# Attention cores of a transformer kernel: ScalarE exponentiates one head of eight straight from PSUM, VectorE shifts the other seven

## The chip, the cores and the metric

One core of a Trainium2 chip runs the whole program. The metric is the device time of one launch, in microseconds (us). The engines are TensorE (PE, with its weight loads shown apart as PEld), VectorE (DVE), ScalarE (ACT), GpSimd (POOL) and SyncE (SP). They run beside each other and are ordered only by semaphores. Each works its own instructions in program order.

## What is computed

The program takes 16 sequences of 128 tokens with 256 features through four layers. Each layer has an attention-like step and a feed-forward step. Two of the attention steps, that of layer 0 (causal self-attention, 4 key/value groups for 16 heads) and that of layer 1 (cross-attention to the context, 16 heads), use the function that is changed. Cut to what matters, with 16 heads of 16 features each:

```
scores = einsum('bqhd,bkhd->bhqk', q, k) / sqrt(16)      # layer 0 adds a causal mask of -1e9
attn   = softmax(scores, axis=-1)
out    = einsum('bhqk,bkhd->bqhd', attn, v)
```

The softmax is computed with the row's maximum subtracted before the exponential.

## The kernel before

`attention_core` is called twice: with the tag `l0a` and `causal=True` (the layer-0 stage, about 97 to 216 us of the span) and with the tag `l1a` and `causal=False` (the layer-1 stage, about 712 to 816 us). One call walks through 32 steps, `h` = 0 to 31. A step is half of one sequence's heads: 8 heads, each a 128x128 block of scores, 1024 columns in two PSUM banks. Steps alternate between two pairs of banks (`both(h)`, `bank(h, half)`).

For a step, in the order of the data:

- GpSimd writes `KBD` (L525): the keys of one chunk, repeated four times and multiplied by a 0/1 mask of heads, `C_HEAD`.
- TensorE, `scores(h)`: in the causal stage two matmuls that put the mask into the banks (L545), then two products with the queries, recorded as four matmuls (L548). It waits for `KBD` and, as the bank pair is used again every second step, for the shift of step h-2.
- VectorE, `largest(h)` (L609): the negated maximum of each head into `NM`. `shift(h)` (L616): scores plus that, from PSUM into the SBUF tile `E` (a ring of four).
- ScalarE: the exponential in place in `E` (L666), with the scale 1/4.
- TensorE, `turn(h)`: eight transposes of `E` into PSUM (L558). ScalarE, `copy(h)` (L651): these out of PSUM into `PT`. TensorE, `values(h)` (L572): 16 small matmuls with the values.
- Once for two steps: ScalarE `columns(b)` (L657) copies the sums out of PSUM, TensorE `turn_rows(b)` (L584) transposes them, VectorE `sums` (L624) and `norm` (L629) divide.

The order on each engine is written out by hand. It is what the work around the change hangs on:

- TensorE, iteration h: `scores(h)`; on even h from 6 on `turn_rows((h-6)/2)`; `turn(h-3)`; `values(h-4)`.
- VectorE, iteration h: `largest(h)`, [`sums`], `shift(h)`, [`norm`]; the ones in brackets on even h.
- ScalarE, iteration h: `copy(h-2)`; on even h from 4 on `columns((h-4)/2)`; the exponential of h.

So on ScalarE the exponential of step h-2 stands behind `copy(h-4)`, which waits for `turn(h-4)`; and on TensorE `turn(h-4)` and `values(h-5)` are the last things before `scores(h)`.

Of the kernel before, what the change touches and what calls it, by code (L numbers as in the profile page):

```python
# [23 lines left out]
P = 128  # L24
# [29 lines left out]
def shape_constants():  # L54

    c = np.zeros((P, C_END), np.float32)
    t = np.arange(P)
    c[:, C_IDENT:C_IDENT + P] = np.eye(P)
    lag = t[None, :] - t[:, None]
    c[:, C_DECAY:C_DECAY + P] = np.where(lag >= 0, DECAY ** np.maximum(lag, 0).astype(np.float64), 0.0)  # L60
    half = D // 2
    power = 10000.0 ** (np.arange(half, dtype=np.float32) / np.float32(half)).astype(np.float64)
    theta = np.float32(1.0) / power.astype(np.float32)
    ang = t[:, None].astype(np.float32) * theta[None, :].astype(np.float32)
    c[:, C_COS:C_COS + half] = np.cos(ang.astype(np.float64))
    c[:, C_SIN:C_SIN + half] = np.sin(ang.astype(np.float64))
    c[:, C_CAUSAL:C_CAUSAL + P] = np.where(t[None, :] > t[:, None], NEG_CAUSAL, 0.0)
    c[:, C_LESS:C_LESS + P] = t[:, None] < t[None, :]
    c[:, C_HEAD:C_HEAD + 4] = (t[:, None] % 64) // DH == np.arange(4)[None, :]
    c[:, C_IOTA:C_IOTA + 16] = np.arange(16)[None, :]  # L70
    c[:, C_ROW:C_ROW + 8] = (t[:, None] % 64 - np.arange(8)[None, :]) / 8.0
    return c
# [16 lines left out]
def build(nc, I, out):  # L89
# [20 lines left out]
    with top:  # L110
# [381 lines left out]
        def attention_core(tag, QT, KT, V, AO, groups, causal):  # L492
# [5 lines left out]

            with ExitStack() as c:
                ER, PR, KR = 4, 2, 3  # L500
                KBD = sb_in(c, f"{tag}_KBD", [P, KR, 4, P])
                E = sb_in(c, f"{tag}_E", [P, ER, 2 * BANK])
                PT = sb_in(c, f"{tag}_PT", [P, PR, 2 * BANK])
# [14 lines left out]
                with nc.Block() as block:  # L518
# [14 lines left out]
                    @block.tensor  # L533
                    def _(pe):
                        if causal:
                            pe.wait_ge(s_cm, 1)

                        def scores(h):
                            b, chunk = h // 2, h % 2
                            pe.wait_ge(s_kbd, h + 1)  # L540
                            if h >= 2:
                                pe.wait_ge(s_shift, h - 1)
                            if causal:
                                for half in range(2):
                                    nc.tensor.matmul(bank(h, half), IDB[:, :], CM[:, :, :], start=True, stop=False)  # L545
                            for half in range(2):
                                rows = slice(64 * half, 64 * half + 64)
                                ins = nc.tensor.matmul(bank(h, half), QT[rows, chunk, b * S:(b + 1) * S],  # L548
                                                       KBD[rows, h % KR, :, :], start=not causal, stop=True)
                            ins.then_inc(s_s, 1)  # L550

                        def turn(h):

                            pe.wait_ge(s_exp, h + 1)
                            if h >= 1:
                                pe.wait_ge(s_pt, h)
                            for n in range(8):
                                ins = nc.tensor.transpose(TP[:, n * P:(n + 1) * P],  # L558
                                                          E[:, h % ER, n * P:(n + 1) * P], IDENT)
                            ins.then_inc(s_turn, 1)  # L560

                        def values(h):

                            b, chunk = h // 2, h % 2
                            pe.wait_ge(s_pt, h + 1)
                            if h == 0:
                                pe.wait_ge(s_clear, 1)
                            if chunk == 0 and b >= 1:
                                pe.wait_ge(s_os, b)
                            for n in range(8):  # L570
                                head, slot, at = 8 * chunk + n, 2 * chunk + n // 4, 32 * (n % 4)
                                ins = nc.tensor.matmul(OT[at:at + DH + 1, slot * P:(slot + 1) * P],  # L572
                                                       V[:, b, head * groups // NH, :],
                                                       PT[:, h % PR, n * P:(n + 1) * P],
                                                       start=True, stop=True, skip_group_check=True)
                            ins.then_inc(s_pv, 1)

                        def turn_rows(b):

                            pe.wait_ge(s_os, b + 1)  # L580
                            if b >= 1:
                                pe.wait_ge(s_ao, b)
                            for slot in range(4):
                                ins = nc.tensor.transpose(PS[:, 7, slot * P:(slot + 1) * P],  # L584
                                                          OS[:, slot * P:(slot + 1) * P], IDENT)
                            ins.then_inc(s_row, 1)

                        for h in range(STEPS + 5):
                            if h < STEPS:
                                scores(h)  # L590
                            if h >= 6 and h % 2 == 0:
                                turn_rows((h - 6) // 2)
                            if 3 <= h < STEPS + 3:
                                turn(h - 3)
                            if 4 <= h < STEPS + 4:
                                values(h - 4)

                    @block.vector
                    def _(dve):
                        nc.vector.memset(OT, 0.0).then_inc(s_clear, 1)  # L600
                        if causal:
                            nc.vector.tensor_copy(
                                CM[:, :, :], CONST[:, C_CAUSAL:C_CAUSAL + P].rearrange("p (o s) -> p o s", o=1)
                                .broadcast_to([P, 4, P])).then_inc(s_cm, 1)

                        def largest(h):

                            dve.wait_ge(s_s, h + 1)
                            nc.vector.tensor_reduce(NM[:, h % ER, :], both(h), AX, ALU.max, negate=True).then_inc(s_max, 1)  # L609

                        def shift(h):

                            dve.wait_ge(s_max, h + 1)
                            if h >= ER:
                                dve.wait_ge(s_turn, h - ER + 1)
                            nc.vector.tensor_tensor(  # L616
                                E[:, h % ER, :].rearrange("p (g s) -> p g s", s=P), both(h),
                                NM[:, h % ER, :].rearrange("p (g o) -> p g o", o=1).broadcast_to([P, 8, P]),
                                ALU.add).then_inc(s_shift, 1)

                        def sums(b):

                            dve.wait_ge(s_row, b + 1)
                            nc.vector.reciprocal(RD[:, b % 2, :], O[:, :, DH]).then_inc(s_rd, 1)  # L624

                        def norm(b):

                            dve.wait_ge(s_rd, b + 1)
                            nc.vector.tensor_tensor(  # L629
                                AO[:, b, :].rearrange("p (h e) -> p h e", e=DH), O[:, :, 0:DH],  # L630
                                RD[:, b % 2, :].rearrange("p (h o) -> p h o", o=1).broadcast_to([P, NH, DH]),
                                ALU.mult).then_inc(s_ao, 1)

                        for h in range(STEPS):
                            largest(h)
                            if h % 2 == 0 and h >= 6:
                                sums((h - 6) // 2)
                            shift(h)
                            if h % 2 == 0 and h >= 6:
                                norm((h - 6) // 2)  # L640
                        for b in range((STEPS - 8) // 2 + 1, B):
                            sums(b)
                            norm(b)

                    @block.scalar
                    def _(act):
# [12 lines left out]
                        for h in range(STEPS + 4):  # L659
# [3 lines left out]
                                columns((h - 4) // 2)  # L663
                            if h < STEPS:
                                act.wait_ge(s_shift, h + 1)
                                nc.scalar.activation(E[:, h % ER, :], E[:, h % ER, :], ACT.Exp,  # L666
                                                     scale=DH ** -0.5).then_inc(s_exp, 1)


        def l0_attention():  # L670
# [3089 lines left out]
```

## Time and profile before

| | us |
|---|---|
| median of 3 runs (lowest, highest) | 1597.98 (1592.46, 1606.96) |
| the profiled execution: its own time | 1595.48 |
| its span, first to last instruction | 1593.7 |
| PE, DVE, ACT, POOL busy in the span | 1323.9, 1131.5, 909.3, 719.7 |
| mean granted TensorE clock | 0.912 of full speed |

A time is that of a whole launch; a span is that of the instructions alone. Busy time is summed over the engine's instructions and says nothing of what waits for what; that is read from the stretches in order of time.

### The profile page before, as it was taken

The page shows a single profiled execution, that of the slowest core. Times are in us where ns is not written, and L with a number is a line of the kernel's source. Part 1 is how long each engine was busy: PE and PEld are TensorE (multiplying, and loading weights), DVE is VectorE, ACT ScalarE, POOL GpSimd, SP SyncE. Part 2 cuts the span into 40 slices and gives each one's busy share as a digit, 9 for nine tenths or more (in the row PEclk, how much of TensorE's full clock was granted, in tenths as well). Part 3 has the DMA queues.
Part 4 walks back from the last instruction along what each step waited for, and adds up shares of the span by engine and source line. Part 5 has one row for each costly group of instructions (what it writes and reads, how often), then busy time and mean ns, then how long its engine had stood idle before and what let it go on. Part 6 is the DMA issues. An engine that isn't in the chain of part 4 may idle for free. (4 is left out here: it accounts for less than half of the span.)

```text
span 1593.7 us, 28302 instructions
## 1 busy us (share of the span) xinstructions
PE 1323.9 (83%) x9642; PEld 1110.3 (70%) x9642; DVE 1131.5 (71%) x2469; ACT 909.3 (57%) x1952; POOL 719.7 (45%) x753
## 2 busy tenths in 40 slices
PE   2699977899999999879984679999778965656898
PEld 0445565799999999735564579999776841345687
DVE  6447756688888988559965647898565658785654
ACT  3236652677777877557732348778426357464432
POOL 2223201467766776513320128888402940453444
PEclk8699997999999999899995789999899988676999
DMA  5000003556657666220012216777511000101000
GB/s 187 1 1 1 1 11 118 193 206 262 253 220 267 243 238 256 93 96 1 1 54 93 80 52 247 253 251 251 186 35 54 1 0 1 34 1 62 1 27 27
DMA packets 60780, 173.69 MB, mean 109 GB/s; under 512 B 10256, under 2 KB 42000, under 8 KB 51040
## 3 DMA queue, kind: packets, MB, share of 16 engines
q1 hardware_dynamic: 53152, 151.42, 26.6%
q0 software_dynamic: 7488, 20.46, 3.7%
q8 instruction: 81, 1.33, 0.4%
q14 instruction: 59, 0.48, 0.1%
HBM read 155.34 MB, written 16.52 MB: 108 GB/s over the span
## 5 line engine op out<-in xcount | busy, mean ns | idle before, releaser
L1812 POOL TENSOR_TENSOR l0m_e_DL<-l0m_e_DN,l0m_e_DH 128x256 fp32r<-128x256 f32 x192 | 175.2, 922 | 96.6 <-ACT l0m_e_DH L1655 95.2
L1720 DVE TENSOR_TENSOR l0m_e_UL<-l0m_e_U,l0m_e_UH 128x512 fp32r<-128x512 f32 x192 | 168.7, 884 | 10.9 <-ACT l0m_e_UH L1645 10.4
L1581 PE MATMUL PS<-l0m_e_CH,l0m_e_UH 128*128 128x256 f32 x480 | 138.4, 288 | 2.0 <-DVE l0m_e_CL L1755 2.0
L1581 PE MATMUL PS<-l0m_e_CL,l0m_e_UH 128*128 128x256 f32 x480 | 136.5, 284 | 0.0
L1581 PE MATMUL PS<-l0m_e_CH,l0m_e_UL 128*128 128x256 f32 x480 | 136.5, 284 | 0.0
L1645 ACT CAST l0m_e_UH<-l0m_e_U 128x512 fp32r<-128x512 f32 x192 | 117.9, 615 | 0.0
L1812 POOL TENSOR_TENSOR l1m_e_DL<-l1m_e_DN,l1m_e_DH 128x256 fp32r<-128x256 f32 x96 | 86.9, 921 | 16.6 <-ACT l1m_e_DH L1655 15.5
L1581 PEld LDWEIGHTS PS<-l0m_e_CH,l0m_e_UH 128*128 128x128 f32 x480 | 92.7, 193 | 2.2 <-ACT l0m_e_UH L1645 2.2
L1581 PEld LDWEIGHTS PS<-l0m_e_CH,l0m_e_UL 128*128 128x128 f32 x480 | 92.8, 193 | 0.0
L1581 PEld LDWEIGHTS PS<-l0m_e_CL,l0m_e_UH 128*128 128x128 f32 x480 | 92.8, 193 | 0.0
L1614 PE MATMUL PS<-l0m_e_DH,l0m_e_HH 128*128 128x256 f32 x312 | 89.0, 285 | 4.5 <-issue 2.6
L1720 DVE TENSOR_TENSOR l1m_e_UL<-l1m_e_U,l1m_e_UH 128x512 fp32r<-128x512 f32 x96 | 83.1, 868 | 11.2 <-ACT l1m_e_UH L1645 10.7
L1614 PE MATMUL PS<-l0m_e_DH,l0m_e_HL 128*128 128x256 f32 x312 | 88.6, 284 | 0.0
L1614 PE MATMUL PS<-l0m_e_DL,l0m_e_HH 128*128 128x256 f32 x312 | 88.5, 284 | 0.0
L1655 ACT CAST l0m_e_DH<-l0m_e_DN 128x256 fp32r<-128x256 f32 x192 | 77.8, 406 | 0.2 <-PE PS L1614 0.2
L3505 POOL TENSOR_TENSOR Z<-l3f_WI,Z 128x512 f32<-128x512 f32 x32 | 50.6, 1584 | 59.9 <-DVE Z L3601 54.9
L525 POOL TENSOR_TENSOR l0a_KBD<-l0a_KT,CONST 128x512 f32<-128x512 f32 x32 | 33.4, 1045 | 91.4 <-PE PS L548 62.6
L525 POOL TENSOR_TENSOR l1a_KBD<-CTX,CONST 128x512 f32<-128x512 f32 x32 | 33.1, 1039 | 91.7 <-PE PS L548 48.8
L1734 DVE SCALAR_TENSOR_TENSOR Z<-PS,l0m_e_BU,Z 128x256 f32<-128x256 f32 x120 | 57.3, 478 | 24.2 <-ACT Z L1664 23.8
L1581 PE MATMUL PS<-l1m_e_CH,l1m_e_UH 128*128 128x256 f32 x240 | 70.9, 295 | 2.2 <-DVE l1m_e_CL L1755 1.5
L1746 DVE TENSOR_TENSOR l0m_e_HL<-Z,l0m_e_HH 128x256 fp32r<-128x256 f32 x120 | 70.5, 588 | 0.0
L1664 ACT ACTIVATE Z<-PS,l0m_e_BU 128x256 f32<-128x256 f32 x120 | 56.9, 474 | 23.1 <-PE PS L1581 21.0
(610 smaller groups left out, 4753.5 us busy)
## 6 DMA issues: line engine op xcount, KB each, us to landing
l0m_e_U<-in_l_up SPq DMA_DIRECT2D x24, 2048.0 KB
l0m_e_DN<-in_l_down SPq DMA_DIRECT2D x24, 1024.0 KB
l1m_e_U<-in_l_up SPq DMA_DIRECT2D x24, 1024.0 KB, 6.3
l1m_e_DN<-in_l_down SPq DMA_DIRECT2D x24, 512.0 KB, 3.9
CTX<-in_ctx SPq DMA_DIRECT2D x2, 2048.0 KB, 10.3
l1a_GA<-results_by_choice SPq DMA_DIRECT2D x16, 256.0 KB, 6.0
l1m_c_GA<-results_by_choice SPq DMA_DIRECT2D x16, 256.0 KB, 4.3
Z<-in_l_b_rows SPq DMA_DIRECT2D x24, 128.0 KB, 3.0
```

Of the source, the lines that this page charges most:

```text
L525: nc.gpsimd.tensor_tensor(KBD[:, h % KR, :, :], KT[:, chunk, b * S:(b + 1) * S].rearrange("p (o s) -> p o s", o=1) .broadcast_to([P, 4, S] ...
L1581: ins = nc.tensor.matmul(hb(u)[:, a * SLOTS:(a + 1) * SLOTS], w[:, f % RING, k, a, :], x[:, t % 2, k, :], start=(p == 0), stop=(p == len(p ...
L1614: ins = nc.tensor.matmul(yb(t)[:, r, :], h[:, t % 2, f, r * P:(r + 1) * P], w[:, f % RING, :], start=(f == 0 and r == 0 and p == 0), stop= ...
L1645: nc.scalar.copy(UH[:, f % RING, :, :, :], U[:, t % 2, :, :, f * P:(f + 1) * P]).then_inc(s_uh, 1)
L1655: nc.scalar.copy(DH[:, f % RING, :], DN[:, t % 2, f, :]).then_inc(s_dh, 1)
L1664: ins = nc.scalar.activation(SG[:, u % 4, :], hb(u)[:, 0:SLOTS], ACT.Silu, **kw)
L1720: nc.vector.tensor_tensor(UL[:, f % RING, :, :, :], U[:, t % 2, :, :, f * P:(f + 1) * P], UH[:, f % RING, :, :, :].bitcast(F32), ALU.subtr ...
L1734: ins = nc.vector.scalar_tensor_tensor(out=HR[:, u % 4, :], in0=hb(u)[:, SLOTS:2 * SLOTS], scalar=BU[:, t % 2, 1, f:f + 1], in1=SG[:, u % ...
L1746: ins = nc.vector.tensor_tensor(HL[:, t % 2, f, :], HR[:, u % 4, :], HH[:, t % 2, f, :].bitcast(F32), ALU.subtract)
L1812: nc.gpsimd.tensor_tensor(DL[:, f % RING, :], DN[:, t % 2, f, :], DH[:, f % RING, :].bitcast(F32), ALU.subtract).then_inc(s_dl, 1)
L3505: nc.gpsimd.tensor_tensor(HR(u), HA(u), HB(u), ALU.add).then_inc(s_h, 1)
```

## The change

ScalarE now makes two instructions of the exponential of a step. The first takes the last of the eight heads directly from its PSUM bank, with the negated maximum as its bias (128 columns). The second takes the seven heads that VectorE has shifted (896 columns), in place in `E` as before. VectorE's shift covers seven heads. Both ScalarE instructions stand behind the same wait for the shift of the step, and in the same place of ScalarE's order. The scale 1/4 moves out of the exponential into the head mask `C_HEAD`, and so into `KBD`. Each step counts two on `s_exp`: `turn(h)` waits for both. Since ScalarE now reads the score banks too, `scores(h)` has a second condition for using them again: the first of the two ScalarE instructions of step h-2.

```diff
--- before.py
+++ after.py
@@ -66,7 +66,7 @@
     c[:, C_SIN:C_SIN + half] = np.sin(ang.astype(np.float64))
     c[:, C_CAUSAL:C_CAUSAL + P] = np.where(t[None, :] > t[:, None], NEG_CAUSAL, 0.0)
     c[:, C_LESS:C_LESS + P] = t[:, None] < t[None, :]
-    c[:, C_HEAD:C_HEAD + 4] = (t[:, None] % 64) // DH == np.arange(4)[None, :]
+    c[:, C_HEAD:C_HEAD + 4] = ((t[:, None] % 64) // DH == np.arange(4)[None, :]) * DH ** -0.5
     c[:, C_IOTA:C_IOTA + 16] = np.arange(16)[None, :]
     c[:, C_ROW:C_ROW + 8] = (t[:, None] % 64 - np.arange(8)[None, :]) / 8.0
     return c
@@ -498,6 +498,7 @@
 
             with ExitStack() as c:
                 ER, PR, KR = 4, 2, 3
+                SHIFTED = 7
                 KBD = sb_in(c, f"{tag}_KBD", [P, KR, 4, P])
                 E = sb_in(c, f"{tag}_E", [P, ER, 2 * BANK])
                 PT = sb_in(c, f"{tag}_PT", [P, PR, 2 * BANK])
@@ -540,6 +541,7 @@
                             pe.wait_ge(s_kbd, h + 1)
                             if h >= 2:
                                 pe.wait_ge(s_shift, h - 1)
+                                pe.wait_ge(s_exp, 2 * (h - 2) + 1)
                             if causal:
                                 for half in range(2):
                                     nc.tensor.matmul(bank(h, half), IDB[:, :], CM[:, :, :], start=True, stop=False)
@@ -551,7 +553,7 @@
 
                         def turn(h):
 
-                            pe.wait_ge(s_exp, h + 1)
+                            pe.wait_ge(s_exp, 2 * (h + 1))
                             if h >= 1:
                                 pe.wait_ge(s_pt, h)
                             for n in range(8):
@@ -614,8 +616,8 @@
                             if h >= ER:
                                 dve.wait_ge(s_turn, h - ER + 1)
                             nc.vector.tensor_tensor(
-                                E[:, h % ER, :].rearrange("p (g s) -> p g s", s=P), both(h),
-                                NM[:, h % ER, :].rearrange("p (g o) -> p g o", o=1).broadcast_to([P, 8, P]),
+                                E[:, h % ER, 0:SHIFTED * P].rearrange("p (g s) -> p g s", s=P), both(h)[:, 0:SHIFTED, :],
+                                NM[:, h % ER, 0:SHIFTED].rearrange("p (g o) -> p g o", o=1).broadcast_to([P, SHIFTED, P]),
                                 ALU.add).then_inc(s_shift, 1)
 
                         def sums(b):
@@ -663,8 +665,10 @@
                                 columns((h - 4) // 2)
                             if h < STEPS:
                                 act.wait_ge(s_shift, h + 1)
-                                nc.scalar.activation(E[:, h % ER, :], E[:, h % ER, :], ACT.Exp,
-                                                     scale=DH ** -0.5).then_inc(s_exp, 1)
+                                nc.scalar.activation(E[:, h % ER, SHIFTED * P:8 * P], both(h)[:, SHIFTED, :], ACT.Exp,
+                                                     bias=NM[:, h % ER, SHIFTED:8]).then_inc(s_exp, 1)
+                                nc.scalar.activation(E[:, h % ER, 0:SHIFTED * P], E[:, h % ER, 0:SHIFTED * P],
+                                                     ACT.Exp).then_inc(s_exp, 1)
 
 
         def l0_attention():
```

## Rows read from the trace of the kernel before

**Rows 1.** The page, busy time (share of the span) and instructions of each engine.
```profile
PE 1323.9 (83%) x9642; PEld 1110.3 (70%) x9642; DVE 1131.5 (71%) x2469; ACT 909.3 (57%) x1952; POOL 719.7 (45%) x753
```

**Rows 2.** Windows: stretch, length, then busy time and instruction count of each engine; 15 us of either stage.
```profile
140.00:155.00 15.00, 15.00 (x146) 7.82 (x138) 11.69 (x14) 10.25 (x12) 4.16 (x4) 1.00 0.00 1
740.00:755.00 15.00, 15.00 (x170) 9.00 (x158) 13.81 (x17) 11.67 (x14) 5.20 (x5) 1.00 0.01 2
```

**Rows 3.** Timeline of the layer-0 stage: start, duration, engine, line, operation [idle before, releaser].
```profile
149.78 1.01 ACT L651 COPY l0a_PT<-PS 128x1024 f32<-128x1024 f32 x1 [1.22 <-PE PS L558]
150.03 1.23 DVE L616 TENSOR_TENSOR l0a_E<-PS,l0a_NM 128x1024 f32<-128x1024 f32 x1
...
150.24 0.60 PE L545 MATMUL PS<-l0a_CM,IDB 128*128 128x512 bf16 x2
150.69 0.59 ACT L657 COPY l0a_OS<-PS 128x512 f32<-128x512 f32 x1
...
151.17 1.07 ACT L666 ACTIVATE l0a_E<-l0a_E 128x1024 f32<-128x1024 f32 x1
...
153.40 1.01 ACT L651 COPY l0a_PT<-PS 128x1024 f32<-128x1024 f32 x1 [1.16 <-PE PS L558]
...
153.86 0.60 PE L545 MATMUL PS<-l0a_CM,IDB 128*128 128x512 bf16 x2
154.31 1.06 ACT L666 ACTIVATE l0a_E<-l0a_E 128x1024 f32<-128x1024 f32 x1
...
156.58 1.01 ACT L651 COPY l0a_PT<-PS 128x1024 f32<-128x1024 f32 x1 [1.22 <-PE PS L558]
```

**Rows 4.** Timeline of the layer-1 stage, two steps.
```profile
754.50 1.01 ACT L651 COPY l1a_PT<-PS 128x1024 f32<-128x1024 f32 x1 [0.66 <-PE PS L558]
...
754.95 1.13 PE L548 MATMUL PS<-l1a_KBD,l1a_QT 64*128 64x512 f32 x4
755.41 1.06 ACT L666 ACTIVATE l1a_E<-l1a_E 128x1024 f32<-128x1024 f32 x1
...
757.14 1.01 ACT L651 COPY l1a_PT<-PS 128x1024 f32<-128x1024 f32 x1 [0.68 <-PE PS L558]
...
757.60 1.13 PE L548 MATMUL PS<-l1a_KBD,l1a_QT 64*128 64x512 f32 x4
...
758.53 1.07 ACT L666 ACTIVATE l1a_E<-l1a_E 128x1024 f32<-128x1024 f32 x1
...
758.77 1.23 DVE L609 TENSOR_REDUCE l1a_NM<-PS 128x8 f32<-128x1024 f32 x1 [0.16 <-PE PS L548]
...
760.26 1.01 ACT L651 COPY l1a_PT<-PS 128x1024 f32<-128x1024 f32 x1 [0.66 <-PE PS L558]
```

**Rows 5.** Groups by line and shape, ScalarE: count, busy us, mean ns, idle before.
```profile
L3100 ACT ACTIVATE l3a_E<-PS,l3a_NM 128x128 f32<-128x128 f32 x16 | 6.0, 373 | 10.2 <-DVE l3a_NM L3160 10.2
...
L2500 ACT ACTIVATE l2a_E<-PS,l2a_NM 128x128 f32<-128x128 f32 x16 | 5.7, 356 | 7.1 <-DVE l2a_NM L2604 7.1
...
L2509 ACT COPY l2a_ET<-PS 128x128 f32<-128x128 f32 x16 | 4.0, 247 | 1.7 <-PE PS L2338 1.7
```

**Rows 6.** Timeline, end of the layer-0 stage: a TensorE wait that ScalarE ended.
```profile
210.47 0.59 ACT L657 COPY l0a_OS<-PS 128x512 f32<-128x512 f32 x1
...
211.12 0.66 PE L584 MATMUL PS<-CONST,l0a_OS 128*128 128x128 f32 x4 [1.03 <-ACT l0a_OS L657]
```

**Rows 7.** Windows: end of the layer-0 stage, start of the layer-1 stage; granted clock after POOL.
```profile
208.00:212.00 4.00, 2.51 (x32) 2.09 (x33) 0.19 (x1) 2.78 (x4) 0.00 (x0) 1.00 0.01 2
720.00:724.00 4.00, 4.00 (x16) 2.04 (x14) 3.93 (x4) 1.29 (x2) 1.04 (x1) 0.57 0.00 0
```

**Rows 8.** Timeline, start of the layer-1 stage, at the lower clock.
```profile
719.77 1.72 PE L548 MATMUL PS<-l1a_KBD,l1a_QT 64*128 64x512 f32 x4 [1.26 <-POOL l1a_KBD L525]
...
723.42 1.01 ACT L651 COPY l1a_PT<-PS 128x1024 f32<-128x1024 f32 x1 [2.71 <-PE PS L558]
```

## The prediction

> **What bounds the kernel now.** I read the page first: TensorE is busy 83% of the span, VectorE 71%, ScalarE 57% [rows 1]. That is a mean over stages, so the windows of the two stages that call the changed function come next. In both TensorE is busy for all of its 15.00 us, while VectorE has 11.69 (layer 0) and 13.81 us (layer 1), ScalarE 10.25 and 11.67 us [rows 2]. A busy TensorE could still be a modelled one, so the timeline has to confirm it. Over two steps of layer 0, `values` of the step before runs straight into `scores`, and this into `turn`: from one `copy` to the second one after it are 156.58 - 149.78 = 6.80 us [rows 3]; in layer 1 they are 760.26 - 754.50 = 5.76 us [rows 4]. The old wait of `scores(h)` never holds it: the mask matmuls start at 153.86, and the shift that they depend on started at 150.03 and took 1.23 us, so it had been done for 2.60 us [rows 3]. VectorE waits for TensorE, not the other way, though in layer 1 by only 0.16 us in the step shown [rows 4]. So both stages run at TensorE's own pace, with ScalarE answering in between.
>
> The point to see is where ScalarE stands at that moment. At 153.86 TensorE begins `scores(h)`. ScalarE is then in the middle of `copy(h-4)` (153.40 to 154.41) and begins the exponential of step h-2 at 154.31, 0.45 us after TensorE has begun to overwrite the banks of step h-2 [rows 3]. This is allowed today, since that exponential reads `E`. In the step before it is worse: scores begin at 150.24, the exponential, behind `copy` and `columns`, at 151.17, 0.93 us later [rows 3]. In layer 1 the same two gaps are 755.41 - 754.95 = 0.46 and 758.53 - 757.60 = 0.93 us [rows 4].
>
> **The change part by part.** *The shift of seven heads.* At most an eighth of 1.23 us, 0.15 us a step, on an engine with slack: 0 on the path. If TensorE's cover were gone and VectorE set the pace, it would be a gain; that is a rival below.
>
> *The scale in the head mask.* The same GpSimd instruction with other numbers, and the causal mask is exact after the move too: 0.
>
> *The second exponential instruction.* ScalarE gets one more fixed cost a step. The direct one is 128x128 from PSUM with a bias from SBUF. The trace has the same form twice, 373 and 356 ns, and a bare copy of that shape at 247 ns [rows 5]. I take 0.36, the row without a difference in form that I can name; the ends are 0.25 and 0.37. ScalarE has room for it: two of them in 5.76 us on top of 11.67/15 busy. It costs only what hangs on its end.
>
> *The new wait, which decides.* `scores(h)` now waits for the direct instruction of h-2, which stands behind `copy(h-4)` and every second time behind `columns`. `copy(h-4)` itself can't begin before `turn(h-4)` ends, and `turn(h-4)` stands behind `scores(h-1)` on TensorE. So a ring closes over both engines, once a step: scores, turn, copy, (columns), direct, next scores. Behind the waiting scores stand `turn_rows`, `turn(h-3)` and `values(h-4)`; the next `copy` waits for that turn. Only `values(h-5)` still fits beside it, under `copy`. The ring's length:
>
> - Layer 0, scores with `turn_rows` behind them: from the scores' start to `copy`'s start 153.40 - 150.24 = 3.16; `copy`'s start to the next ScalarE start 154.31 - 153.40 = 0.91; direct 0.36; then TensorE's start after a ScalarE end, 211.12 - (210.47 + 0.59) = 0.06 [rows 3, 5, 6]. Sum 4.49 us.
> - Layer 0, the other step: 156.58 - 153.86 = 2.72; with `columns` in between 151.17 - 149.78 = 1.39; 0.36; 0.06 [rows 3]. Sum 4.53. The pair 9.02 against 6.80: +2.22 us.
> - Layer 1: 760.26 - 757.60 = 2.66, 0.91, 0.42: 3.99; and 757.14 - 754.95 = 2.19, 758.53 - 757.14 = 1.39, 0.42: 4.00 [rows 4]. The pair 7.99 against 5.76: +2.23 us.
>
> By the code the ring is closed for `scores(4)` to `scores(31)`, 28 of 32: before that ScalarE has no copy ahead of its exponential. 14 pairs make 14 x 2.22 = 31.1 us in layer 0 and 14 x 2.23 = 31.2 in layer 1. `scores(2)` and `scores(3)` wait for VectorE today; they gain up to 0.15 and pay 0.36, and the last exponentials are longer by about 0.28: 0.4 us a stage, 0.8 for both. VectorE and GpSimd fall behind nobody, since they work less often. Sum +63.1 us.
>
> The Trainium skill ("ScalarE: Activation LUTs", What ACT_TABLE_LOAD costs) gives an ACTIVATE with a pointer bias 280 ns + 0.833 ns per column, an estimate of 387 ns for 128 columns, and lets neighbours overlap by about 93 ns; the rows agree on the overlap (next start 0.10 us before the end) and have 356 and 373 ns for the duration. By the page's figure the sum would be 1.5 us more.
>
> The profiled execution took 1595.48 us, so it would take 1658.6. The median of the runs shown is 2.5 us above it. I predict **1661 us**, 3.9% slower.
>
> **The rivals.** *The wait is free and VectorE's saving shows (not slower).* This is the case if the direct instruction of h-2 is done when `values(h-5)` ends. It would need an end 0.45 + 0.36 = 0.81 us earlier than the rows give it; from then on TensorE's pace is the old one. If VectorE sets the pace in layer 1, then 32 x 0.15 = 4.8 us are saved: 1593; if not, the time stays at 1598. For: VectorE's idle time in layer 1 is small [rows 4]. Against: ScalarE takes its instructions in the written order, and in the rows its exponential starts after the scores in each of the four steps [rows 3, 4]. Chance 0.04.
>
> *The change does less than it says:* the direct instruction is as cheap as the bare copy and part of the wait was idle anyway. 56 waits x 0.11 = 6 us less: 1655. Inside the forecast's range, with it 0.84.
>
> *The clock falls.* TensorE would now idle about 2.2 us in each 9.0 and each 8.0 us. For it: at the start of layer 1, after idle stretches of 1.26 us and more, the granted clock of 720 to 724 us is 0.57, near the lower level of 1.2 GHz [rows 7, 8]. Against it: at the end of layer 0 the same instructions with waits of 1.03 us in between, TensorE busy 2.51 of 4.00 us, kept a granted clock of 1.00, the level of 2.4 GHz [rows 6, 7]; the new loop would be denser than that. The price: at the lower clock scores start to copy start is 723.42 - 719.77 = 3.65 us instead of 2.19 [rows 4, 8], so +1.46 a step. For all 56 steps 82 us: 1743. For a quarter of them 20 us: 1681. Chance 0.12.
>
> **How the numbers follow.** Forecast 0.84, clock 0.12, free wait 0.04. The three runs shown reach 5.5 us below and 9 us above their median. Low end: 1661 - 6 - 5 = 1650. High end: 1661 + 9 for the spread, and room for a quarter of the steps at the low clock: 1683. What is left out is the free wait and the worse half of the clock's rival, near 0.1, and a tenth for an error of size in the ring. A measurement of this kernel can tell about 1% from no change, 16 us. Faster by more than that: 0.01, from the rival with VectorE's saving and something unseen. Within 1%: 0.03. Slower: 0.96.
>
> **What the new profile would show.** Right: TensorE's `scores` (L545 in layer 0, L548 in layer 1) with idle time before them, 0.9 to 1.4 us each, ended by ScalarE's direct exponential; steps of 4.5 and 4.0 us; a span some 31 us longer in either stage and nothing anywhere else; 64 ScalarE instructions of 128x128 at 0.36 us; VectorE's wait for scores longer by the same amount, its shift shorter by 0.1 to 0.15. Wrong: scores that start before the exponential as now (the free wait), or a granted clock under 1.00 within the stages (the clock). Most of all it would be wrong if something let `copy` start earlier than the end of the turn, since the whole ring hangs on that.

## The result, and the profile after

The changed kernel took 1670.1 us (median of 4 runs, 1666.63 to 1674.01) against 1597.32 us. The ratio is 1.045, 95% interval 1.039 to 1.051. The change made the kernel 4.5% slower; 1661 us had been forecast, with a range of 1650 to 1683.

The page, busy time of each engine, over a span of 1672.1 us (1593.7 before):
```profile
PE 1335.3 (80%) x9624; PEld 1122.5 (67%) x9642; DVE 1115.2 (67%) x2469; ACT 917.1 (55%) x2016; POOL 722.2 (43%) x753
```
TensorE's busy time is 11.4 us more than in [rows 1], for the same work; VectorE's is 16 us less. Neither sum explains 78 us. The windows of 15 us in the two stages (same columns as [rows 2]) do:
```profile
155.00:170.00 15.00, 10.83 (x100) 6.07 (x104) 7.67 (x10) 8.07 (x13) 3.12 (x3) 1.00 0.00 1
770.00:785.00 15.00, 10.43 (x115) 6.18 (x113) 9.24 (x12) 9.36 (x14) 3.46 (x4) 1.00 0.00 1
```
TensorE was busy for all of its 15 us in either stage; now it is for 10.83 and 10.43 us. The granted clock is 1.00 here too. So TensorE was idle for 28 to 30% of these stretches, at full clock. The groups of the layer-0 stage name what it waited for:
```profile
L611 DVE TENSOR_REDUCE l0a_NM<-PS 128x8 f32<-128x1024 f32 x32 | 39.2, 1224 | 61.5 <-PE PS L550 61.5
...
L618 DVE TENSOR_TENSOR l0a_E<-PS,l0a_NM 128x896 f32<-128x896 f32 x32 | 34.3, 1072 | 0.7
...
L547 PE MATMUL PS<-l0a_CM,IDB 128*128 128x512 bf16 x49 | 16.5, 394 | 38.7 <-ACT l0a_E L668 32.5 <-DVE l0a_E L618 2.6 <-DVE l0a_CM L604 2.3
L668 ACT ACTIVATE l0a_E<-PS,l0a_NM 128x128 f32<-128x128 f32 x32 | 12.0, 376 | 7.4 <-DVE l0a_E L618 7.4
```
The shift became shorter, 1072 ns (1.23 us in the timeline before), and the direct exponential is 376 ns. But the mask matmuls, which open `scores`, stood idle before them for 38.7 us, 32.5 of them ended by that same direct exponential (L668), and VectorE's `largest` waited 61.5 us for scores. The timeline of one pair of steps in layer 0 shows the ring:
```profile
149.51 1.01 ACT L653 COPY l0a_PT<-PS 128x1024 f32<-128x1024 f32 x1 [2.46 <-PE PS L560]
...
150.41 0.37 ACT L668 ACTIVATE l0a_E<-PS,l0a_NM 128x128 f32<-128x128 f32 x1
...
150.90 0.13 PEld L547 LDWEIGHTS PS<-l0a_CM,IDB 128*128 128x128 bf16 x2 [1.15 <-issue]
...
153.64 1.01 ACT L653 COPY l0a_PT<-PS 128x1024 f32<-128x1024 f32 x1 [2.02 <-PE PS L560]
...
154.55 0.59 ACT L659 COPY l0a_OS<-PS 128x512 f32<-128x512 f32 x1
155.03 0.38 ACT L668 ACTIVATE l0a_E<-PS,l0a_NM 128x128 f32<-128x128 f32 x1
...
155.52 0.13 PEld L547 LDWEIGHTS PS<-l0a_CM,IDB 128*128 128x128 bf16 x2 [1.64 <-issue]
155.55 0.59 PE L547 MATMUL PS<-l0a_CM,IDB 128*128 128x512 bf16 x2 [1.39 <-ACT l0a_E L668]
...
158.70 1.01 ACT L653 COPY l0a_PT<-PS 128x1024 f32<-128x1024 f32 x1 [2.46 <-PE PS L560]
```
Read it from `copy` to `copy`. The copy starts at 149.51, the direct exponential at 150.41, TensorE's first weight load of `scores` at 150.90; a turn later the next copy starts, 153.64. Then copy, `columns`, direct (155.03), TensorE at 155.52, and the third copy at 158.70. On ScalarE each instruction starts 0.10 to 0.12 us before the end of the one ahead of it; TensorE's weight load starts 0.11 to 0.12 us after the direct exponential ends. The pair takes 9.19 us, 6.80 in [rows 3]. Layer 1 does the same:
```profile
770.72 1.01 ACT L653 COPY l1a_PT<-PS 128x1024 f32<-128x1024 f32 x1 [1.93 <-PE PS L560]
...
771.63 0.37 ACT L668 ACTIVATE l1a_E<-PS,l1a_NM 128x128 f32<-128x128 f32 x1
...
772.14 1.13 PE L550 MATMUL PS<-l1a_KBD,l1a_QT 64*128 64x512 f32 x4 [0.90 <-ACT l1a_E L668]
...
774.33 1.01 ACT L653 COPY l1a_PT<-PS 128x1024 f32<-128x1024 f32 x1 [1.50 <-PE PS L560]
...
775.24 0.59 ACT L659 COPY l1a_OS<-PS 128x512 f32<-128x512 f32 x1
775.72 0.38 ACT L668 ACTIVATE l1a_E<-PS,l1a_NM 128x128 f32<-128x128 f32 x1
...
776.25 1.13 PE L550 MATMUL PS<-l1a_KBD,l1a_QT 64*128 64x512 f32 x4 [1.39 <-ACT l1a_E L668]
...
778.87 1.01 ACT L653 COPY l1a_PT<-PS 128x1024 f32<-128x1024 f32 x1 [1.93 <-PE PS L560]
```
From 770.72 to 778.87 are 8.15 us, 5.76 in [rows 4], with idle stretches of 0.90 and 1.39 us before the scores.

In sum the layer-0 stage (first `KBD` to last `norm`) went from 118.2 to 152.8 us and the layer-1 stage from 102.6 to 136.2: 34.6 + 33.6 = 68.2 of the 78.4 us. The other 10.2 us lie elsewhere, 9.4 of them behind the layer-1 stage (778.6 to 788.0 us); a repeat, below, decides whether they belong to the change.

### The profile page after: what moved, and what is told of

Read it like the earlier page. It is cut to its first block and busy times, and to the rows that moved or that the text cites. A ratio compares the mean times of both kernels' runs of the same rounds, so it can differ in the third digit from the quotient of the medians.

```text
span 1672.1 us, 28348 instructions
## 1 busy us (share of the span) xinstructions
PE 1335.3 (80%) x9624; PEld 1122.5 (67%) x9642; DVE 1115.2 (67%) x2469; ACT 917.1 (55%) x2016; POOL 722.2 (43%) x753
## 5 line engine op out<-in xcount | busy, mean ns | idle before, releaser
L1724 DVE TENSOR_TENSOR l0m_e_UL<-l0m_e_U,l0m_e_UH 128x512 fp32r<-128x512 f32 x192 | 163.5, 857 | 11.0 <-ACT l0m_e_UH L1649 10.4
L1585 PE MATMUL PS<-l0m_e_CL,l0m_e_UH 128*128 128x256 f32 x480 | 136.7, 285 | 0.0
L1585 PE MATMUL PS<-l0m_e_CH,l0m_e_UL 128*128 128x256 f32 x480 | 136.7, 285 | 0.0
L1724 DVE TENSOR_TENSOR l1m_e_UL<-l1m_e_U,l1m_e_UH 128x512 fp32r<-128x512 f32 x96 | 75.1, 786 | 20.4 <-ACT l1m_e_UH L1649 17.1
L611 DVE TENSOR_REDUCE l0a_NM<-PS 128x8 f32<-128x1024 f32 x32 | 39.2, 1224 | 61.5 <-PE PS L550 61.5
```

Source lines behind the costliest of these rows:

```text
L1585: ins = nc.tensor.matmul(hb(u)[:, a * SLOTS:(a + 1) * SLOTS], w[:, f % RING, k, a, :], x[:, t % 2, k, :], start=(p == 0), stop=(p == len(p ...
L1724: nc.vector.tensor_tensor(UL[:, f % RING, :, :, :], U[:, t % 2, :, :, f * P:(f + 1) * P], UH[:, f % RING, :, :, :].bitcast(F32), ALU.subtr ...
```

## The experiments

The theory: the new wait closes a ring of scores, turn, copy, (columns), direct exponential and next scores, because the direct exponential stands behind `copy` on ScalarE. Its rivals: the split itself costs (a second instruction, a PSUM read by ScalarE); the wait costs wherever it stands; VectorE's time is worth something; the clock falls. All times are medians; the kernel before, on the same chips, had medians of 1597 to 1600 us.

**The wait without the rest.** The kernel before, plus one line:

```diff
                                 pe.wait_ge(s_shift, h - 1)
+                                pe.wait_ge(s_exp, h - 1)
```

> The kernel before with one line more: scores(h) also waits for the exponential of step h-2, which is still the whole 128x1024 one in place. Nothing else of the change. Ring theory: the same ring over TensorE and ScalarE closes, with an exponential of 1.07 us in it in place of the direct one of 0.37, so 56 x 0.70 = 39 us more than the changed kernel: 1709 us. Rival, the cost lies in the second ScalarE instruction or in its read of PSUM: about 1597, since neither is here.

Measured: 1724.78 us, ratio 1.078 (1.072 to 1.083). One wait, and nothing else of the change, costs more than the whole change, since the exponential in the ring is now the full one:
```profile
151.58 1.07 ACT L667 ACTIVATE l0a_E<-l0a_E 128x1024 f32<-128x1024 f32 x1
...
152.79 0.59 PE L546 MATMUL PS<-l0a_CM,IDB 128*128 128x512 bf16 x2 [2.08 <-ACT l0a_E L667]
...
156.85 1.06 ACT L667 ACTIVATE l0a_E<-l0a_E 128x1024 f32<-128x1024 f32 x1
...
158.06 0.59 PE L546 MATMUL PS<-l0a_CM,IDB 128*128 128x512 bf16 x2 [1.59 <-ACT l0a_E L667]
```
Each scores start follows the end of a full exponential (1.06 to 1.07 us long) by 0.14 to 0.15 us. The stage of layer 0 took 177.1 us, 24.3 more than with the change, and layer 1 took 168.6, 32.4 more, where 28 x 0.70 = 19.6 had been expected for each. So some 17 us lie above the ring's length, 5 in layer 0 (granted clock 0.95 over the stage, 0.98 with the change) and 13 in layer 1. The windows of layer 1 show what goes with them:
```profile
840.00:850.00 10.00, 6.34 (x64) 3.60 (x62) 5.26 (x6) 4.42 (x5) 2.08 (x2) 1.00 0.01 2
870.00:880.00 10.00, 7.50 (x60) 4.37 (x60) 5.26 (x6) 3.41 (x5) 2.08 (x2) 0.83 0.00 0
```
The granted clock of this stage switches between its two levels: 1.00 in one stretch, and in another 0.83, which is the mean of a stretch that was partly at either level (0.89 over the stage). This is what the prediction's third rival had, but for a sparser loop than the change's.

**The split without the wait.** VectorE shifts all eight heads, ScalarE makes its two instructions in `E`, so that no one but VectorE reads the scores:

```diff
-                                pe.wait_ge(s_exp, 2 * (h - 2) + 1)
...
-                                E[:, h % ER, 0:SHIFTED * P].rearrange("p (g s) -> p g s", s=P), both(h)[:, 0:SHIFTED, :],
-                                NM[:, h % ER, 0:SHIFTED].rearrange("p (g o) -> p g o", o=1).broadcast_to([P, SHIFTED, P]),
+                                E[:, h % ER, :].rearrange("p (g s) -> p g s", s=P), both(h),
+                                NM[:, h % ER, :].rearrange("p (g o) -> p g o", o=1).broadcast_to([P, 8, P]),
...
-                                nc.scalar.activation(E[:, h % ER, SHIFTED * P:8 * P], both(h)[:, SHIFTED, :], ACT.Exp,
-                                                     bias=NM[:, h % ER, SHIFTED:8]).then_inc(s_exp, 1)
+                                nc.scalar.activation(E[:, h % ER, SHIFTED * P:8 * P], E[:, h % ER, SHIFTED * P:8 * P],
+                                                     ACT.Exp).then_inc(s_exp, 1)
```

> The changed kernel without the PSUM read and so without the new wait: VectorE shifts all eight heads, ScalarE still makes two instructions (128 columns and 896), both in place in E, and the scale stays in the head mask. Ring theory: TensorE sets the pace again and ScalarE has room for 0.28 us more a step, 1597 us within the spread of runs. Rival, the second instruction costs its fixed part on the path: 64 x 0.28 = 18 us, 1615.

Measured: 1598.68 us, ratio 1.000 (0.997 to 1.003). The second instruction and the scale in the mask cost nothing that can be measured.

**The whole change, in another order on ScalarE.**

```diff
                         for h in range(STEPS + 4):
-                            if 2 <= h < STEPS + 2:
-                                copy(h - 2)
-                            if h >= 4 and h % 2 == 0:
-                                columns((h - 4) // 2)
                             if h < STEPS:
                                 act.wait_ge(s_shift, h + 1)
...
+                            if 2 <= h < STEPS + 2:
+                                copy(h - 2)
+                            if h >= 4 and h % 2 == 0:
+                                columns((h - 4) // 2)
```

This is called the open order below.

> The changed kernel with all its parts, but in each ScalarE iteration the two exponentials of h stand ahead of copy(h-2) and columns. Ring theory: the direct instruction of h-2 no longer stands behind a copy that waits for turn(h-4), so the ring is open and the wait of scores(h) is met before it is asked: TensorE's pace, 1597 us, less what VectorE saves at the two ends, at most 5 us: 1592 to 1598. Rival, the wait itself or two readers of the PSUM banks cost something wherever they stand: near 1670, or clearly above 1600.

Measured: 1598.37 us, ratio 0.9995 (0.997 to 1.002). Every part of the change is in it, the wait and the PSUM read too, and the 70 us are gone. In layer 0:
```profile
151.53 1.01 ACT L653 COPY l0a_PT<-PS 128x1024 f32<-128x1024 f32 x1 [1.01 <-PE PS L560]
...
152.47 0.37 ACT L664 ACTIVATE l0a_E<-PS,l0a_NM 128x128 f32<-128x128 f32 x1
...
154.71 1.01 ACT L653 COPY l0a_PT<-PS 128x1024 f32<-128x1024 f32 x1 [1.04 <-PE PS L560]
...
155.17 0.61 PE L547 MATMUL PS<-l0a_CM,IDB 128*128 128x512 bf16 x2
...
156.10 0.38 ACT L664 ACTIVATE l0a_E<-PS,l0a_NM 128x128 f32<-128x128 f32 x1
```
The direct exponential at 152.47 is the one that the scores at 155.17 wait for: it ends 2.3 us before they start. It still follows a copy on ScalarE, that of 151.53, but an older one, which TensorE doesn't hold back. From this copy to the next are 154.71 - 151.53 = 3.18 us, as from 153.40 to 156.58 in [rows 3].

**The same order in the kernel before**, as a control.

```diff
-                            if 2 <= h < STEPS + 2:
-                                copy(h - 2)
-                            if h >= 4 and h % 2 == 0:
-                                columns((h - 4) // 2)
                             if h < STEPS:
...
+                            if 2 <= h < STEPS + 2:
+                                copy(h - 2)
+                            if h >= 4 and h % 2 == 0:
+                                columns((h - 4) // 2)
```

> The kernel before with only the order of ScalarE changed, the exponential of h ahead of copy(h-2) and columns. The control for the same order in the changed kernel. TensorE sets the pace of both orders: 1597 us, no difference over 1%. If the order alone gains or loses in the stages, this shows how much of the other run is the order's.

Measured: 1597.91 us, ratio 0.9985 (0.996 to 1.001). The order alone is worth nothing.

**The direct exponential ahead of `columns`, still behind `copy`.**

```diff
                             if 2 <= h < STEPS + 2:
                                 copy(h - 2)
-                            if h >= 4 and h % 2 == 0:
-                                columns((h - 4) // 2)
                             if h < STEPS:
                                 act.wait_ge(s_shift, h + 1)
                                 nc.scalar.activation(E[:, h % ER, SHIFTED * P:8 * P], both(h)[:, SHIFTED, :], ACT.Exp,
                                                      bias=NM[:, h % ER, SHIFTED:8]).then_inc(s_exp, 1)
+                            if h >= 4 and h % 2 == 0:
+                                columns((h - 4) // 2)
+                            if h < STEPS:
                                 nc.scalar.activation(E[:, h % ER, 0:SHIFTED * P], E[:, h % ER, 0:SHIFTED * P],
                                                      ACT.Exp).then_inc(s_exp, 1)
```

> The changed kernel with the direct exponential ahead of columns, but still behind copy. Ring theory: columns (0.48 us from start to the next start) leaves the ring in every second step, 28 x 0.48 = 13 us less: 1657. If the ring were not what sets the time, the place of columns would change nothing: 1670.

Measured: 1656.01 us, ratio 1.036 (1.031 to 1.041). Against the change the stages are 6.1 and 6.0 us shorter, 12 of the 13 us expected: `columns` was a link of the ring in every second step.

**One more link: two heads taken directly.** Each step counts three on `s_exp`.

```diff
-                SHIFTED = 7
+                SHIFTED = 6
...
-                                pe.wait_ge(s_exp, 2 * (h - 2) + 1)
+                                pe.wait_ge(s_exp, 3 * (h - 2) + 2)
...
-                            pe.wait_ge(s_exp, 2 * (h + 1))
+                            pe.wait_ge(s_exp, 3 * (h + 1))
...
-                                nc.scalar.activation(E[:, h % ER, SHIFTED * P:8 * P], both(h)[:, SHIFTED, :], ACT.Exp,
-                                                     bias=NM[:, h % ER, SHIFTED:8]).then_inc(s_exp, 1)
+                                for g in range(SHIFTED, 8):
+                                    nc.scalar.activation(E[:, h % ER, g * P:(g + 1) * P], both(h)[:, g, :], ACT.Exp,
+                                                         bias=NM[:, h % ER, g:g + 1]).then_inc(s_exp, 1)
```

> The changed kernel with two heads taken directly (two ScalarE instructions of 128 columns), VectorE shifts six, and scores(h) waits for the second of them. Ring theory: one more instruction in the ring at 0.27 us from start to start, 56 x 0.27 = 15 us more: 1685. Rival, VectorE's work counts: another 0.13 us a step less on VectorE, 1670 less 8.

Measured: 1681.06 us, ratio 1.054 (1.046 to 1.061); the stages are 6.5 and 9.8 us longer, 16 in sum. 28 x 0.27 = 7.6 for each stage, 15 in sum, had been expected; the 2 us more in layer 1 go with a lower clock at the start of that stage (0.73 and 0.76 in the two stretches of 10 us from 760 us on, 1.00 from 780 us to its end). The medians are 11 us (first comparison) and 13 us (the repeat below) above the changed kernel's. VectorE had still less to do, and the time rose by about the ring's length.

**The redundant wait.**

```diff
-                                pe.wait_ge(s_shift, h - 1)
                                 pe.wait_ge(s_exp, 2 * (h - 2) + 1)
```

> The changed kernel without scores(h)'s wait for the shift of h-2, which the wait for the direct exponential already contains (ScalarE waits for that shift before it). The trace of the changed kernel starts TensorE 0.11 to 0.15 us after the direct instruction ends, not 0.06. If the third condition in a row costs this, 56 x 0.06 = 3.4 us less: 1666. If not: 1670.

Measured: 1668.1 us, ratio 1.041 (1.036 to 1.047). The stages took 152.1 and 137.1 us, as with the change, and TensorE's weight load still started 0.12 us after the direct instruction ended. The third condition isn't what makes the start late; two are left, and no run has `scores` with one.

**Three heads taken directly** (`SHIFTED = 5`, four on `s_exp` for each step, edited like `two_direct`), to see the clock in a loop as sparse as that of the first experiment, made in another way.

> The changed kernel with three heads taken directly, VectorE shifts five, scores(h) waits for the third; ScalarE's order as in the changed kernel. The step of layer 1 becomes about 4.1 + 2 x 0.27 = 4.6 us, as long as in wait_alone (4.8), where the granted clock of that stage fell to 0.89. Ring theory alone: 56 x 0.54 = 30 us more than the changed kernel, 1700 us, the clock as there. If TensorE's idle share is what brings the clock down, whatever causes it: a granted clock clearly under 0.99 in the layer-1 stage here too, and some 10 us more, 1710.

Measured: 1712.86 us, ratio 1.070 (1.066 to 1.073). Layer 0 kept its clock and took 14.7 us more than with the change, the 28 x 0.54 = 15 of the ring. Layer 1 took 29.1 us more, at a granted clock of 0.88. TensorE in that stage:
```profile
821.21 1.13 PE L550 MATMUL PS<-l1a_KBD,l1a_QT 64*128 64x512 f32 x4 [1.90 <-ACT l1a_E L669]
...
822.76 1.04 PE L560 MATMUL PS<-CONST,l1a_E 128*128 128x128 f32 x8
...
830.40 1.14 PE L550 MATMUL PS<-l1a_KBD,l1a_QT 64*128 64x512 f32 x4 [1.90 <-ACT l1a_E L669]
...
832.37 1.91 PE L560 MATMUL PS<-CONST,l1a_E 128*128 128x128 f32 x8
```
The same eight transposes take 1.04 us at 822.76 and 1.91 us at 832.37. The windows of these stretches:
```profile
820.00:830.00 10.00, 5.86 (x60) 3.51 (x60) 4.47 (x6) 6.15 (x15) 2.08 (x2) 1.00 0.00 0
830.00:840.00 10.00, 7.42 (x60) 4.79 (x60) 4.46 (x6) 4.84 (x10) 2.08 (x2) 0.83 0.01 2
```
Within the second of them the granted clock was 0.50 from 832 to 834 us and 1.00 again from 835 us on.

**Two direct heads in the open order**, the edits of `two_direct` and `exp_first` together.

> Two direct heads, VectorE shifts six, and in each ScalarE iteration the exponentials stand ahead of copy and columns, so the ring is open. If only the ring costs: 1597, although ScalarE has 2 x 0.27 us a step more than in the kernel before. If VectorE's work were worth something in layer 1, 0.25 us a step less would give 32 x 0.25 = 8 us less: 1589. If ScalarE's room is used up (2.4 of 2.9 us a step in layer 1), it would be longer than 1600.

Measured: 1598.37 us, ratio 0.999 (0.997 to 1.001). ScalarE had room for two more instructions a step, and a quarter of the shift taken from VectorE gained nothing. None of these versions beats the kernel before by an amount that can be measured.

**The changed kernel once more**, with no edit.

> The changed kernel itself once more. The two stages took 68.2 us of its 78.4 us more of span; 9.4 us lay behind the layer-1 stage, most of them at the lower clock at the start of the last layer. If that is the state of the clock on entry and not the change: the stages again 34.6 and 33.6 us longer than before, and behind them either about 778 or about 788 us. If the change lengthens the last layer: 788 each time.

Measured: 1667.71 us, ratio 1.042 (1.039 to 1.045), now 68.3 us over the kernel before. The stages took 150.7 and 136.7 us, 66.6 together above before, and behind them 779.7 us. The start of the last layer in the first profile of the change and in this one:
```profile
1539.00:1553.00 14.00, 14.00 (x50) 12.43 (x49) 0.50 (x1) 1.79 (x3) 0.59 (x1) 0.50 0.00 1
```
```profile
1539.00:1553.00 14.00, 13.06 (x72) 10.90 (x70) 6.29 (x38) 5.54 (x10) 3.20 (x3) 0.98 0.01 2
```
TensorE had waited 24 us for a transfer up to 1513 us, and in both the granted clock was 0.50 from 1535 to 1539 us. In the first it stayed at 0.50 for these 14 us; in the second it was 1.00 from 1540 us on, 0.98 over the stretch, and TensorE got through 72 matmuls in place of 50. From ScalarE's first write of `l3f_WI` there to GpSimd's first sum with it are 14.0 us in the one, 8.0 in the other, and 8.1 before. Among the other kernels only the one without the redundant wait had 14.1. So the changed kernel has these 6 us in one execution and not in another: they are no fixed cost of the change. Whether they are commoner with it isn't known. Two of the three profiles of the changed and the one-wait-less kernel have them, none of the nine others, and each profile is a single execution. What the remaining 3 us behind the layer-1 stage were isn't settled; all but 1 us of them are absent in the repeat.

## Why the prediction was right

*What bounds the stages.* TensorE's own pace, as read from its unbroken timeline. Shown from two sides: VectorE relieved of an eighth and of a quarter of its shift in the open order gave nothing, and ScalarE with one or two instructions more cost nothing. No run took work from TensorE itself, so that it is TensorE's pace rests on its unbroken timeline and on the exclusion of the others.

*The shift, the scale, the second instruction at zero.* All three held; the split without the wait and the whole change in the open order are both at the kernel before's time. The direct instruction measured 376 ns, where 0.36 was taken and 0.37 was the upper end.

*The new wait.* It is the cost, all of it. The wait alone brings it back, the open order with the wait takes it away, and the links that were added or taken out moved the two stages by about their own length (`columns` -12, one more direct +16). The parts of the ring that were read off the old timeline as differences of starts came out to within 0.01 us on ScalarE: copy to direct 0.90 (0.91), with columns 1.39 (1.39).

*The size.* The ring was forecast at 9.02 and 7.99 us a pair and measured 9.19 and 8.15. The term that was mis-sized is the last one: TensorE's start after ScalarE's end, taken as 0.06 us from `turn_rows`. From the direct one's start to the scores' first matmul are 0.51 to 0.53 us, where 0.36 + 0.06 had been put. Of these 0.10 us a step about 0.02 are the direct instruction's (376 ns) and 0.08 the start; the other links were 0.03 to 0.04 us a pair shorter than read. In sum a pair was 0.17 us longer in layer 0 and 0.16 in layer 1, 14 x 0.33 = 4.6 us: 63.1 + 4.6 = 67.7, and the stages measured 68.2 and, the second time, 66.6. The trace of before had the better row, the first scores that wait for VectorE:
```profile
103.61 1.22 DVE L616 TENSOR_TENSOR l0a_E<-PS,l0a_NM 128x1024 f32<-128x1024 f32 x1
...
104.95 0.13 PEld L545 LDWEIGHTS PS<-l0a_CM,IDB 128*128 128x128 bf16 x2 [1.84 <-issue]
104.98 0.59 PE L545 MATMUL PS<-l0a_CM,IDB 128*128 128x512 bf16 x2 [1.04 <-DVE l0a_E L616]
```
The shift ends at 104.83, the weight load starts 0.12 and the matmul 0.15 us later: the very instructions that would have to wait, after a wait. I had taken the delay from other instructions. Why `scores` starts later after a release than `turn_rows` does stays open; taking one of its three conditions away changed nothing. The old trace has both values elsewhere too: the transposes at 208.47 start 0.15 us after the end of the copy that releases them (207.31 + 1.01), the `values` at 213.75 0.05 us after theirs (212.69 + 1.01).

*The free wait and VectorE's saving (1593 to 1598).* Its condition wasn't met by the written order, as argued. The open order shows that the condition was the right one: with the direct exponential done early the time is 1598, and even then without a saving.

*The clock.* It didn't fall with the change: 0.98 and 0.99 over the two stages of the first profile, 1.00 and 0.96 of the second, the dips being at the start of a stage. But the rival was nearer than its 12% made it look. With idle stretches of 1.42 and 1.90 us in steps of some 4.6 us layer 1 ran at 0.88, while the change has 0.90 and 1.39 in steps of some 4.1. The price was some 13 to 14 us for the stage (32.4 - 19.6, and 29.1 - 15), well below the 41 us of a stage at the lower clock throughout.

*The rest of the difference.* About 6 of the 78.4 us between the two profiled executions went with a low clock on entry to the last layer, which the prediction had only as the spread of the runs. The four times of the changed kernel lie in two pairs, near 1667 and near 1673.5, and the repeat's median is 1667.7. The forecast of 1661 was 9 us low against the first median and 7 against the second. Both lie inside the range, whose upper part was made for spread and for a lower clock in the two stages; the clock there was not what brought the time up.

## What to carry to other kernels

Before an engine is allowed to read a shared buffer, ask what stands ahead of that read in the engine's own order, and whether that waits for the engine that will reuse the buffer: if it does, two engines that overlapped take turns. Such a ring can be summed from the old timeline by differences of starts, and it is opened by order: a shorter ring is still a ring (without `columns` it gave back 12 of 68 us here, the order all of them). Work taken from an engine that isn't the last to arrive buys nothing, so look first whether it has any idle time that ends on someone else.

## What was not expected of the hardware

- Between one loop and the next sparser one the granted clock of layer 1 fell. At 4.07 us a step, with TensorE idle 0.90 and 1.39 us before the scores, it is 1.00 once the stage has started; with two direct heads, at 4.34 us a step, idle 1.16 and 1.65, still 1.00 from 780 us on. At some 4.6 us a step, idle 1.42 and 1.90, it is 0.83 to 1.00 in turn, 0.88 over the stage; at some 4.8, idle 1.59 and 2.08 (`wait_alone`), 0.89 over the stage. A longer exponential and more of them did it alike. Layer 0, which has the bf16 mask matmuls besides, kept 1.00 within the stage with three direct heads, but in `wait_alone` it too showed 0.83, from 160 to 180 us.
- The start of an instruction after a release is not one number on TensorE: 0.06 us for `turn_rows`, 0.12 to 0.15 us for `scores`, after VectorE and after ScalarE alike.
- A direct exponential of 128 columns lasts 376 ns, but the next instruction of ScalarE starts 0.25 to 0.27 us after it did. The bias from SBUF and the source in PSUM don't hinder this overlap of 0.10 to 0.12 us.
